# Feed-forward blocks of a four-layer kernel: a step's down products moved between its gate products and its up products

## The chip, the cores and the metric

One core of one Trainium2 chip runs the whole program. The metric is the device time of one execution in microseconds (us); the kernel before was run three times. The engines are TensorE (PE, with its weight loads as PEld), VectorE (DVE), ScalarE (ACT), GpSimd (POOL) and SyncE (SP), which here only issues DMAs.

## The reference, cut to what matters

The program computes four layers, each a cross-attention and then a feed-forward block, on x of 4 x 256 tokens by 256 features in float32. A feed-forward block is, on the normalised input h,

```python
g = h @ w_gate          # 1024 tokens x width
u = h @ w_up
y = (silu(g) * u * gate_of_the_expert) @ w_down   # layer 3: silu(g * u) for the routed experts
x = x + y
```

Layer 0 is dense with 704 hidden features. Layers 1, 2 and 3 are mixtures in which all experts are computed and laid side by side: 64 experts of 64 features and a shared one (4160), 8 experts of 176 and a shared one of 704 (2112), 16 experts of 176 and a shared one of 176 (2992). An expert's gate is zero where it isn't chosen for a token.

## The kernel before

**Tiles and steps.** The hidden features are cut into chunks of 128: 6, 33, 17 and 24 chunks in the four blocks. The 1024 tokens are cut into two halves of 512. A *step* st is one chunk and one half (c = st // 2, h = st % 2), so the blocks have 12, 66, 34 and 48 steps, 160 in all. Every float32 operand of a product is split into a high and a low float16 part, and a product is hi*hi + lo*hi + hi*lo.

**TensorE** (`pe_ffn`). Per step it issues three groups, all in one queue that runs in order:

- gate products g(st): 6 matmuls of 512 columns (lines 1217 to 1219) into bank h of the accumulator memory; they wait until `s.a` says that VectorE has read the gate products of two steps before;
- up products u(st): 6 matmuls of the same form into bank 2, the only bank for them. They wait until VectorE has read those of the step before (`s.prod`, or `s.a` where the product comes first);
- down products d(st - 8): 12 matmuls of 256 columns (lines 1238 to 1240) that add the hidden features of eight steps before (LAG = 8) into banks 4 to 7. They wait for the low part of these hidden features (`s.lo`) and, at even steps, for the down weights' low part (`s.dn_lo`).

The first eight steps have no down products; the last eight groups of them follow the loop as a tail. So 128 of the 160 groups of down products stand inside the loop.

**VectorE** (`dve_ffn`, `dve_front`) takes in each step st, in this order, with the line of each instruction: a(st) = (tanh + 1) * g (1351); the product with u, m_b (1355); the low part of the next chunk's up weights at even steps (1275), or of the down weights at odd steps (1288); and low(st - 7), the low part of hidden features (1368, or 1370 without an expert gate), which d(st - 7) of the next step waits for. In the first 22 chunks of layer 3 the product comes first: a(st) = g * u (1348), then the weights' part, then, after ScalarE's tanh, m_b (1384), then low(st - 7).

**ScalarE** (`act_ffn`) takes tanh of the gate products (1308; in layer 3 a copy at 1304, and the tanh of a(st) at 1338), the high parts of the weights (1270, 1283) and the high part of the hidden features high(st - 7) (1318, 1321), which waits for the down products that read the same buffer two steps earlier (`s.down`).

**GpSimd** (`pool_ffn`, line 1408) multiplies m_b(st) by the expert's gate into m_c. It waits for m_b(st), for the gates' DMA at even steps, and for low(st - 2), whose buffer it overwrites.

**SyncE** issues the loads in a queue written out by hand: up weights five chunks ahead once `s.up_lo` frees a slot, the rows of gates, the down weights (`sp_ffn`). No planner sets the order; it is the order of the loops above.

Of the kernel before, what the change touches and what calls it, by code (L numbers as in the profile page):

```python
# [36 lines left out]
LAG = 8  # L37
# [47 lines left out]
def build(nc, d, out):  # L85
    ctx = ExitStack()
    with ctx:
# [1063 lines left out]
        def product_first(n, st):  # L1151
            return st // 2 < FFNS[n].first
# [57 lines left out]
        def pe_ffn(n):  # L1210
            pe, s, f = nc.tensor, ffn, FFNS[n]

            def up(c, h, u, to):
                for k in range(KT):
                    w_hi, w_lo = (up_w[:, c % 2, a, (2 * k + u) * P:(2 * k + u + 1) * P] for a in range(2))
                    x_hi, x_lo = (a[:, k, 4 * h:4 * h + 4, :].rearrange("p t c -> p (t c)") for a in (xh, xl))
                    pe.matmul(to, w_hi, x_hi, start=(k == 0), stop=False)  # L1217
                    pe.matmul(to, w_lo, x_hi, start=False, stop=False)  # L1218
                    ins = pe.matmul(to, w_hi, x_lo, start=False, stop=(k == KT - 1))  # L1219
                return ins  # L1220

            def gates_turned():
                pe.wait_ge(s.parts, n)
                for i in range(NT):
                    ins = pe.transpose(PS[0:f.experts, 6 + i // 4, (i % 4) * P:(i % 4 + 1) * P], gates[:, i, 0:f.experts], ident[:])
                ins.then_inc(s.gates_ps, 1)

            def down(st):
                c, h, last = st // 2, st % 2, st >= f.steps - 2
                if h == 0:  # L1230
                    pe.wait_ge(s.dn_lo, f.tiles0 + c + 1)
                pe.wait_ge(s.lo, f.steps0 + st + 1)
                w_hi, w_lo = (dn_w[:, c % 2, a, :] for a in range(2))
                for j in range(4):
                    i = 4 * h + j
                    to = PS[:, 4 + i // 2, (i % 2) * D:(i % 2 + 1) * D]
                    h_hi, h_lo = (hid[:, h, a, j, :] for a in range(2))
                    pe.matmul(to, h_hi, w_hi, start=(c == 0 and i % 2 == 0), stop=False)  # L1238
                    pe.matmul(to, h_hi, w_lo, start=False, stop=False)  # L1239
                    ins = pe.matmul(to, h_lo, w_hi, start=False, stop=(last and i % 2 == 1))  # L1240
                    if last and j == 1:
                        ins.then_inc(s.y_ps, 1)
                if last:
                    ins.then_inc(s.y_ps, 1)
                else:
                    ins.then_inc(s.down, 1)

            for st in range(f.steps):
                c, h = st // 2, st % 2
                if h == 0:  # L1250
                    pe.wait_ge(s.up_lo, f.tiles0 + c + 1)
                if st >= 2:
                    pe.wait_ge(s.a, f.steps0 + st - 1)
                up(c, h, 0, PS[:, h, :]).then_inc(s.g_ps, 1)
                if st >= 1:
                    pe.wait_ge(s.a if product_first(n, st - 1) else s.prod, f.steps0 + st)
                up(c, h, 1, PS[:, 2, :]).then_inc(s.u_ps, 1)
                if st == 3 and f.gated:
                    gates_turned()
                if st == LAG and f.gated:  # L1260
                    pe.wait_ge(s.gates, n)
                if st >= LAG:
                    down(st - LAG)
            for st in range(f.steps - LAG, f.steps):
                down(st)

# [797 lines left out]
        @block.tensor  # L2064
        def _(pe):
            pe_latent(0)
            pe_pre0()
            pe_ffn(0)
            pe_folded(1)
            pe_pre1(1, r1_w, E1 + 1)  # L2070
            pe_ffn(1)
            pe_folded(2)
            pe_pre2()
            pe_ffn(2)
            pe_latent(3)
            pe_pre1(3, r3_w, E3)
            pe_ffn(3)
# [199 lines left out]
```

## Time and profile before

| | |
|---|---|
| median of 3 runs | 1530.09 us (1529.9 to 1530.73) |
| profiled execution, its own time | 1534.58 us |
| its span in the trace | 1532.8 us |
| granted TensorE clock, mean | 0.915 of full speed |
| TensorE busy | 1297.8 us (85%) |
| VectorE busy | 925.9 us (60%) |
| ScalarE busy | 501.6 us (33%) |
| GpSimd busy | 358.9 us (23%) |

The trace is of one execution and its times are us from the span's start. A matmul's recorded duration overlaps the next matmul, so the time that a matmul takes from TensorE is read from start to start. In the timeline a row gives the start, the duration, the engine, the line, the operation, what it writes and reads, and in brackets the idle time before it and what ended it. The granted clock is 1.00 at 2.4 GHz and 0.50 at 1.2 GHz.

### The profile page before, as it was taken

Reading aid. Unit: us, or ns where it says so; the run is one execution under the profiler, and the core shown is the slowest. Engines: PE = TensorE matmul, PEld = TensorE weight load, DVE = VectorE, ACT = ScalarE, POOL = GpSimd, SP = SyncE. Lnnn points to the kernel's source line nnn. Section 1 sums busy time; section 2 is a strip of 40 time slices with the busy share of each in tenths; the row PEclk is TensorE's granted clock in tenths of the full one; section 3 lists DMA queues with packets and bytes.
Section 4 is the critical chain, followed back from the end, with each engine's and each line's share of the span. In section 5 each row is a group of like instructions: output and inputs, shape, how many; then the busy total and the mean of one; then the engine's idle time right before and its main releaser. Section 6 shows DMA issues by size and latency. Waiting matters only on the chain.

```text
span 1532.8 us, 20643 instructions
## 1 busy us (share of the span) xinstructions
PE 1297.8 (85%) x7770; PEld 842.8 (55%) x7772; DVE 925.9 (60%) x1706; ACT 501.6 (33%) x1105; POOL 358.9 (23%) x325
## 2 busy tenths in 40 slices
PE   4658939999879999996997766996999667699998
PEld 2335525799855666654654543565466433456655
DVE  3657665577747666667224448675666655576666
ACT  2322313111123333332221113563333223255553
POOL 0220030366502333333001121000133211123332
PEclk9887969999979999999898878798999977799999
DMA  3010024000024444451330000000234200034442
GB/s 122 1 72 2 27 86 151 1 1 1 1 74 113 116 117 120 121 131 52 117 118 0 0 14 0 1 1 1 81 115 129 94 14 0 1 98 120 121 134 73
DMA packets 41499, 97.53 MB, mean 64 GB/s; under 512 B 5414, under 2 KB 18214, under 8 KB 39360
## 3 DMA queue, kind: packets, MB, share of 16 engines
q1 hardware_dynamic: 41408, 96.31, 20.7%
q8 instruction: 57, 0.93, 0.3%
q14 instruction: 34, 0.28, 0.1%
HBM read 94.88 MB, written 1.42 MB: 63 GB/s over the span
## 4 chain that ended last, share of the span: by engine, by line
PE 61%; issue 21%; DVE 11%; POOL 4%; ACT 3%; DMA 1%; POOLq 0%; SPq 0%; DVEq 0%; ACTq 0%
PE PS L1217 9%; PE PS L1218 9%; PE PS L1219 9%; PE PS L1238 4%; PE PS L1240 4%; PE PS L1239 4%; PE PS L873 3%; POOL arena L323 2%; PE PS L891 2%; PE PS L1826 2%; PE PS L666 2%; PE PS L1843 1%; PE PS L860 1%; PE PS L862 1%; PE PS L861 1%
## 5 line engine op out<-in xcount | busy, mean ns | idle before, releaser
L1408 POOL TENSOR_TENSOR arena<-arena,m_g 128x512 f32<-128x512 f32 x144 | 184.3, 1281 | 441.9 <-DMA m_g<-gate_rows 259.4
L1217 PE MATMUL PS<-arena 128*128 128x512 f16 x640 | 245.8, 384 | 5.1 <-DVE arena L1348 2.2
L1218 PE MATMUL PS<-arena 128*128 128x512 f16 x640 | 245.6, 384 | 0.0
L1219 PE MATMUL PS<-arena 128*128 128x512 f16 x640 | 245.2, 383 | 0.0
L1238 PE MATMUL PS<-arena 128*128 128x256 f16 x640 | 174.5, 273 | 11.9 <-DVE arena L1368 10.2
L1240 PE MATMUL PS<-arena 128*128 128x256 f16 x640 | 174.4, 273 | 0.0
L1239 PE MATMUL PS<-arena 128*128 128x256 f16 x640 | 174.4, 273 | 0.0
L1351 DVE SCALAR_TENSOR_TENSOR arena<-arena,PS 128x512 f32<-128x512 f32 x116 | 79.6, 686 | 133.6 <-ACT arena L1308 133.6
L1308 ACT ACTIVATE arena<-PS 128x512 f32<-128x512 f32 x116 | 69.3, 597 | 263.5 <-PE PS L1219 263.5
L1368 DVE TENSOR_TENSOR arena<-arena 128x512 f16<-128x512 f32 x144 | 114.0, 792 | 2.2 <-ACT arena L1318 2.2
L323 POOL TENSOR_TENSOR arena<-arena,small 128x1024 f32<-128x1024 f32 x24 | 46.2, 1938 | 264.6 <-DVE small L479 264.6
L1219 PEld LDWEIGHTS PS<-arena 128*128 128x128 f16 x640 | 63.3, 99 | 77.6 <-issue 3.6
L1217 PEld LDWEIGHTS PS<-arena 128*128 128x128 f16 x640 | 63.7, 100 | 70.8 <-issue 3.3
L1218 PEld LDWEIGHTS PS<-arena 128*128 128x128 f16 x640 | 63.2, 99 | 62.4 <-issue 2.9
L937 POOL TENSOR_TENSOR arena<-arena 128x256 f32<-128x256 f32 x96 | 67.6, 726 | 125.6 <-DVE arena L965 125.6
L1318 ACT ACTIVATE arena<-arena 128x512 f16<-128x512 f32 x144 | 89.3, 620 | 22.3 <-PE PS L1240 20.7
L1355 DVE TENSOR_TENSOR arena<-arena,PS 128x512 f32<-128x512 f32 x116 | 79.7, 687 | 17.4 <-PE PS L1219 2.7
L1238 PEld LDWEIGHTS PS<-arena 128*128 128x128 f16 x640 | 62.5, 98 | 39.6 <-issue 10.6
L471 DVE TENSOR_REDUCE small<-PS 128x16 f32<-128x1024 f32 x24 | 29.2, 1215 | 85.0 <-PE PS L1012 38.0
L1239 PEld LDWEIGHTS PS<-arena 128*128 128x128 f16 x640 | 62.5, 98 | 20.3
L1240 PEld LDWEIGHTS PS<-arena 128*128 128x128 f16 x640 | 62.6, 98 | 7.3
L1275 DVE SCALAR_TENSOR_TENSOR arena<-w_stage,arena 128x512 f16<-128x512 f32 x80 | 64.2, 807 | 2.8 <-ACT arena L1270 2.8
(251 smaller groups left out, 2358.6 us busy)
## 6 DMA issues: line engine op xcount, KB each, us to landing
w_stage<-in_up SPq DMA_DIRECT2D x80, 256.0 KB, 2.8
m_g<-gate_rows SPq DMA_DIRECT2D x70, 256.0 KB, 4.3
arena<-in_heads SPq DMA_DIRECT2D x16, 1088.0 KB, 5.0
w_stage<-in_down SPq DMA_DIRECT2D x80, 128.0 KB, 4.1
m_g<-gate_rows SPq DMA_DIRECT2D x19, 512.0 KB, 3.8
m_g<-gate_rows SPq DMA_DIRECT2D x6, 448.0 KB, 4.6
m_g<-gate_rows SPq DMA_DIRECT2D x6, 384.0 KB, 4.2
m_g<-gate_rows SPq DMA_DIRECT2D x6, 320.0 KB, 4.0
```

Of the source, the lines that this page charges most:

```text
L323: pool.tensor_tensor(heads_of(at_p[:, q, :]), heads_of(at_p[:, q, :]), over(small[:, q, 2, :], 2, L), ALU.mult).then_inc(norm.pn, 1)
L1217: pe.matmul(to, w_hi, x_hi, start=(k == 0), stop=False)
L1218: pe.matmul(to, w_lo, x_hi, start=False, stop=False)
L1219: ins = pe.matmul(to, w_hi, x_lo, start=False, stop=(k == KT - 1))
L1238: pe.matmul(to, h_hi, w_hi, start=(c == 0 and i % 2 == 0), stop=False)
L1239: pe.matmul(to, h_hi, w_lo, start=False, stop=False)
L1240: ins = pe.matmul(to, h_lo, w_hi, start=False, stop=(last and i % 2 == 1))
L1318: act.activation(hid_part(0, st % 2), m_c[:, st % 2, :], ACT.Copy).then_inc(s.hi, 1)
L1351: dve.scalar_tensor_tensor(a, t, 1.0, g_ps, ALU.add, ALU.mult).then_inc(s.a, 1)
L1355: dve.tensor_tensor(m_b[:, st % LAG, :], a, u_ps, ALU.mult).then_inc(s.prod, 1)
L1368: dve.tensor_tensor(hid_part(1, st % 2), m_c[:, st % 2, :], hid_part(0, st % 2), ALU.subtract).then_inc(s.lo, 1)
L1408: pool.tensor_tensor(m_c[:, st % 2, :], m_b[:, st % LAG, :], m_g[:, st // 2 % 2, st % 2, :], ALU.mult).then_inc(s.c, 1)
```

## The change

In every step of every feed-forward block, the down products of eight steps before are issued between the gate products and the up products, and not after the up products. With them go their waits, and in step 8 the wait for the transposed gates. In step 3 the transposition of the gates keeps its place after the up products. No instruction is added or removed on any engine, and only TensorE's queue is reordered.

```diff
@@ -1252,15 +1252,15 @@
                 if st >= 2:
                     pe.wait_ge(s.a, f.steps0 + st - 1)
                 up(c, h, 0, PS[:, h, :]).then_inc(s.g_ps, 1)
+                if st == LAG and f.gated:
+                    pe.wait_ge(s.gates, n)
+                if st >= LAG:
+                    down(st - LAG)
                 if st >= 1:
                     pe.wait_ge(s.a if product_first(n, st - 1) else s.prod, f.steps0 + st)
                 up(c, h, 1, PS[:, 2, :]).then_inc(s.u_ps, 1)
                 if st == 3 and f.gated:
                     gates_turned()
-                if st == LAG and f.gated:
-                    pe.wait_ge(s.gates, n)
-                if st >= LAG:
-                    down(st - LAG)
             for st in range(f.steps - LAG, f.steps):
                 down(st)
```

## Rows read from the trace of the kernel before

**Rows 1.** Stretches in us: length, busy PE, PEld, DVE, ACT, POOL, clock, DMA share, GB/s.

```profile
475.00:700.00 225.00, 224.66 (x1380) 134.73 (x1378) 146.35 (x231) 87.76 (x173) 76.58 (x60) 1.00 0.45 119
1357.00:1512.00 155.00, 153.77 (x944) 91.98 (x942) 99.46 (x160) 82.88 (x154) 51.44 (x41) 1.00 0.40 120
702.70:717.50 14.80, 11.56 (x96) 8.84 (x96) 13.79 (x15) 4.83 (x10) 7.74 (x6) 1.00 0.22 65
```

**Rows 2.** TensorE's timeline, layer 1, step 41: u, d, next g.

```profile
605.80 0.38 PE L1217 MATMUL PS<-arena 128*128 128x512 f16 x1
...
607.10 0.27 PE L1238 MATMUL PS<-arena 128*128 128x256 f16 x1
...
608.41 0.38 PE L1217 MATMUL PS<-arena 128*128 128x512 f16 x1
```

**Rows 3.** The timeline of VectorE, layer 1, steps 41 and 42.

```profile
606.63 0.69 DVE L1351 SCALAR_TENSOR_TENSOR arena<-arena,PS 128x512 f32<-128x512 f32 x1 [0.77 <-ACT arena L1308]
607.45 0.69 DVE L1355 TENSOR_TENSOR arena<-arena,PS 128x512 f32<-128x512 f32 x1
608.06 0.42 DVE L1288 SCALAR_TENSOR_TENSOR arena<-w_stage,arena 128x256 f16<-128x256 f32 x1
608.39 0.69 DVE L1368 TENSOR_TENSOR arena<-arena 128x512 f16<-128x512 f32 x1
...
611.35 0.69 DVE L1355 TENSOR_TENSOR arena<-arena,PS 128x512 f32<-128x512 f32 x1
611.96 0.68 DVE L1275 SCALAR_TENSOR_TENSOR arena<-w_stage,arena 128x512 f16<-128x512 f32 x1
612.56 0.68 DVE L1368 TENSOR_TENSOR arena<-arena 128x512 f16<-128x512 f32 x1
```

**Rows 4.** TensorE's and VectorE's timelines, layer 3, step 24 (product first).

```profile
1423.61 0.27 PE L1238 MATMUL PS<-arena 128*128 128x256 f16 x1
...
1423.89 0.69 DVE L1348 TENSOR_TENSOR arena<-arena,PS 128x512 f32<-128x512 f32 x1 [1.15 <-PE PS L1219]
...
1425.95 0.68 DVE L1368 TENSOR_TENSOR arena<-arena 128x512 f16<-128x512 f32 x1
```

**Rows 5.** The timeline where layer 1's tail begins: VectorE, TensorE, GpSimd.

```profile
701.99 0.68 DVE L1368 TENSOR_TENSOR arena<-arena 128x512 f16<-128x512 f32 x1
702.87 1.79 DVE L1368 TENSOR_TENSOR arena<-arena 128x512 f16<-128x512 f32 x1 [0.19 <-ACT arena L1318]
...
700.70 0.27 PE L1238 MATMUL PS<-arena 128*128 128x256 f16 x1
...
702.82 0.27 PE L1238 MATMUL PS<-arena 128*128 128x256 f16 x1 [0.65 <-DVE arena L1368]
...
702.85 1.27 POOL L1408 TENSOR_TENSOR arena<-arena,m_g 128x512 f32<-128x512 f32 x1 [2.99 <-DVE arena L1368]
```

**Rows 6.** TensorE's timeline, first down products of layers 1, 0, 3.

```profile
478.40 0.27 PE L1238 MATMUL PS<-arena 128*128 128x256 f16 x1 [0.34 <-DVE arena L1368]
...
165.76 0.27 PE L1238 MATMUL PS<-arena 128*128 128x256 f16 x1
...
1359.14 0.39 PE L1217 MATMUL PS<-arena 128*128 128x512 f16 x1 [0.62 <-DVE arena L1348]
1361.22 0.27 PE L1238 MATMUL PS<-arena 128*128 128x256 f16 x1 [0.61 <-DVE arena L1368]
```

**Rows 7.** VectorE's timeline, layer 0, step 7: the low part.

```profile
164.44 0.69 DVE L1370 SCALAR_TENSOR_TENSOR arena<-arena 128x512 f16<-128x512 f32 x1
```

**Rows 8.** The timeline of VectorE and GpSimd, layer 1, from step 40.

```profile
604.16 1.10 DVE L1275 SCALAR_TENSOR_TENSOR arena<-w_stage,arena 128x512 f16<-128x512 f32 x1
...
610.69 1.28 POOL L1408 TENSOR_TENSOR arena<-arena,m_g 128x512 f32<-128x512 f32 x1 [3.42 <-DMA m_g<-gate_rows]
```

**Rows 9.** TensorE's timeline, layer 0, first gate products.

```profile
140.83 0.63 PE L1218 MATMUL PS<-arena 128*128 128x512 f16 x1
141.26 0.63 PE L1219 MATMUL PS<-arena 128*128 128x512 f16 x1
```

## The prediction, made before the changed kernel was run

> **What bounds the kernel now.** I read the page first (TensorE 85% busy, the others at 60% or less), then the view by stretches of the loops, then the timeline of TensorE and of VectorE side by side over single steps. In the loops TensorE is never without work: 224.66 of 225.00 us in layer 1, 153.77 of 155.00 in layer 3, at the full clock of 2.4 GHz [rows 1]. A step is read from start to start: an up group takes 1.30 us (605.80 to 607.10), a down group 1.31 (607.10 to 608.41) [rows 2], and the gate group, of the same form as the up group, makes the step 3.90, which is also the distance of VectorE's product from step to step (607.45 to 611.35) [rows 3]. No wait inside the loop costs anything, so there is no stall to win back. What must be seen beside this is how late VectorE is. After the up products of an odd step (issued by 607.10) the low part that the *next* down products need starts only at 608.39 and ends at 609.08; after an even step (611.00, one step later) it starts at 612.56 [rows 3]. TensorE does not notice, because between these up products and the down products that read the low part stand d, g and u: 3.91 us.
>
> **The change, part by part.** Work is the same on every engine, and no DMA moves. Between two up groups there are still one d and one g, so the wait for the single up bank has its old cover of 2.61 us. The gate banks' wait has its old cover too. What shrinks is the cover of the down group: between u(st) and d(st - 7), which needs low(st - 7), now stands g(st + 1) alone, 1.30 us. And low(st - 7) stays in VectorE's queue behind the product with u(st). So a circle closes in each step: u ends, VectorE takes the product, a weights' part and the low part, TensorE does d, then u again.
>
> The circle's terms. (a) From u's last slot to VectorE's start: 0.28, as in layer 3 (1423.61 to 1423.89) [rows 4]. In layer 1 it is 0.35 (607.10 to 607.45), but there the product also waits for a(st), which ended at 607.32 [rows 3]; with u 1.31 later a(st) is early, and I take 0.28. The bounds are 0.28 and 0.35. (b) Product to weights' part 0.61; weights' part to low part 0.33 at odd steps (608.06 to 608.39), 0.60 at even ones (611.96 to 612.56) [rows 3]. (c) Start of the low part to the start of the down group that waited for it: 0.83, seen where the tail begins (701.99 to 702.82) [rows 5]. (d) d and u: 2.61. An odd step is then 0.28 + 0.61 + 0.33 + 0.83 + 2.61 = 4.66, 0.76 more than 3.90. An even one is 0.28 + 0.61 + 0.60 + 0.83 + 2.61 = 4.93, 1.03 more. The last even step of a block has no up weights to split: 0.28 + 0.61 + 0.83 + 2.61 = 4.33, 0.43 more. Where the product comes first (layer 3, steps up to 43), ScalarE's tanh lies in the chain, and u's end to the low part's start is 2.34 (1423.61 to 1425.95) [rows 4]: 2.34 + 0.83 + 2.61 = 5.78, 1.88 more. The tail gives a check of the odd chain: from 700.70, where u ended, to 702.82, where a down group waited for the low part, is 2.12 [rows 5]; my sum with 0.35 in place of 0.28 is 2.12.
>
> Counts. The circle runs from u(8) to the last u, in blocks of S steps S - 9 times: 3, 57, 25 and 39. Layer 0: 1.03 + 0.76 + 0.43 = 2.2. Layer 1: 28 x 1.03 + 28 x 0.76 + 0.43 = 50.6. Layer 2: 12 x 1.03 + 12 x 0.76 + 0.43 = 21.9. Layer 3: 36 x 1.88 + 1.03 + 0.76 + 0.43 = 69.9. Together 144.6 us.
>
> The first down group, once per block. In layers 1 and 3 d(0) already waits for its low part (478.40, 1361.22) [rows 6], so it starts when it did. Before, u(8) was already done by then and g(9) came next; now u(8) follows d(0) and ends 2.61 (d and u) after d(0)'s start, the point from which the turns above are counted: +2.61. I take the same for layer 2. In layer 0, d(0) started at 165.76, and its low part at 164.44 would let it start at 165.27: 2.61 - 0.49 = 2.12 [rows 6, 7]. Sum 3 x 2.61 + 2.12 = 10.0. The wait for the gates in step 8 costs nothing: ScalarE copies them in step 4, and d(0) waits longer for its low part. The tail's chain starts at the last u as before, 0.07 earlier by term (a): 0.3 in all four.
>
> **Sum:** 144.6 + 10.0 - 0.3 = +154.3 us. The profiled execution of 1534.58 (its span is 1532.8, 1.8 around it) would become 1688.9; it lies 4.5 above the median of 1530.09, to which I apply the same sum: **1684.4 us**. Other queues: `s.down` now comes before u, so ScalarE's high parts are not later; SyncE's loads follow VectorE's and GpSimd's progress, and a longer step gives them more room. Later layers wait for this one's x, so nothing behind it absorbs the delay.
>
> **A cost that was hidden: VectorE beside GpSimd.** Where the gates' product ran (702.85, 1.27 us), the low part took 1.79 instead of 0.68 [rows 5]; 1275 took 1.10 once [rows 8]. Products that read PSUM stayed at 0.69 [rows 3, 4]. In the loop before, such a hit vanished in the slack; now it would sit on the circle. The Trainium skill has this as a lock ("SBUF — State Buffer", section "SBUF: two separate sides"): a VectorE instruction with two SBUF inputs and a GpSimd one that reads SBUF exclude one another for a whole instruction. The rows agree; the drawn-out 1.79 is such a case. I price it at zero in the sum: GpSimd starts either after the low part that frees its buffer, or 5.43 us after the end of 1275 (605.26 to 610.69) [rows 8]. In the new step, 1275 ends at 0.28 + 0.61 + 0.68 = 1.57, so the gates' product starts at 7.00 after an even u, 2.07 into the next step. That is after its low part (1.22 to 1.90), and GpSimd is done at 3.35, before the next u ends at 4.66. The bound above is 1.11 at every other step.
>
> **Rivals.**
> - *Collisions come back.* If the gates' DMA lands otherwise than I put it, GpSimd's 1.28 us falls on 1275 or the low part. Up to 1.11 x 40 even steps of layers 1 and 2 = +44: 1728 at most, half of it 1706. For it: rows 5 and 8. Against: 2 us of room. Chance 0.08.
> - *The clock falls.* TensorE will rest 1.87 of every 5.78 us in layer 3 (3.17 less g's 1.30) and 0.75 to 1.02 of some 4.8 in the others. In layer 1's tail it was 11.56 of 14.80 us busy, and the clock was granted at 1.00 throughout [rows 1], so I expect full clock. At 1.2 GHz a matmul of 512 columns takes 0.43 (140.83 to 141.26) [rows 9] against 0.217, d and u 5.2 instead of 2.61: 2.6 more per step, +47 if half of layer 3's 36 product-first steps fall there: 1731, and more if other layers join. The Trainium skill states such a rule against this change ("TensorE: Matmul & The Clock Gate", section "A second HAM failure mode: psum-queue depth-cycling"): frequent short idles between groups of matmuls can make the clock swing between its levels. The tail's rows contradict it for its own pattern; no row has 1.87 us of rest in each step. Chance 0.08.
> - *Not slower.* The point is the wait for the low part in front of d: it costs nothing if the low part starts by 1.30 - 0.83 = 0.47 us after u's end. Then g covers it, and only the one wait before u(8) in layer 3 (0.62 [rows 6]) might go: 1529.5, no change. Against: it starts at 1.29 at the earliest [rows 3], and VectorE's order is fixed with the product ahead of it. Chance 0.02.
> - *A circle only partly closed*, with hand-overs shorter than read, or half the steps stalling: +60 to +130, 1590 to 1660. No row supports it. Chance 0.03. That the change does nothing can't be: TensorE's products run in the order written.
>
> **How the numbers follow.** Forecast 0.79, rivals 0.08, 0.08, 0.02, 0.03. Errors of 0.1 us in the circle give 12 us over its 124 turns; with (a) at 0.35 the sum is +163 at most. The lower end allows 0.15 per turn: 1665. The upper end takes in most of the collisions: 1722. A measurement of this kernel can tell 0.2% (3.1 us) from no change. Faster by more than that 0.01, within it 0.02, slower 0.97.
>
> **What would show it.** In the changed profile: TensorE's idle time before line 1238 grows to 120 to 145 us and is ended by 1368; a step in layer 1 lasts 4.66 and 4.93 by turns, in layer 3 5.78; the loops of layers 1 and 3 are 53 and 72 us longer; PEclk stays at 1.00; 1275 and 1368 keep medians of 0.68. The prediction is wrong if the step stays near 3.9, if 1238 waits for something else, or if 1217 to 1219 start 0.43 apart.

## The result and the profile after

| | before | changed |
|---|---|---|
| median | 1530.41 us (4 runs, 1529.90 to 1540.68) | 1675.82 us (4 runs, 1673.69 to 1681.64) |
| profiled execution, its own time | 1534.58 us | 1681.64 us |
| its span | 1532.8 us | 1679.9 us |

The ratio of the changed kernel to the kernel before is 1.0939, with a 95% interval of 1.0884 to 1.0994. The changed kernel is slower by 145 us between the medians, and by 147.1 us between the two profiled executions. The forecast was 154.3 us more, 1684.4 us in all, with a range of 1665 to 1722.

The page of the changed kernel, its costliest groups: where TensorE and VectorE stood idle, and what ended it.

```profile
PE 1321.3 (79%) x7772; PEld 833.6 (50%) x7772; DVE 916.1 (55%) x1706; ACT 498.8 (30%) x1105; POOL 359.7 (21%) x325
...
L1238 PE MATMUL PS<-arena 128*128 128x256 f16 x640 | 174.8, 273 | 136.7 <-DVE arena L1368 131.3
L1217 PE MATMUL PS<-arena 128*128 128x512 f16 x640 | 246.2, 385 | 4.8 <-DVE arena L1427 2.1
...
L1355 DVE TENSOR_TENSOR arena<-arena,PS 128x512 f32<-128x512 f32 x116 | 79.7, 687 | 203.1 <-PE PS L1219 200.7
```

The matmuls cost what they did: 273 and 385 ns each, against 273 and 384 on the page before. What is new is idle time in front of the down products: 136.7 us, of which 131.3 are ended by VectorE's low part (1368). On the page before this entry read 11.9. In turn VectorE's product (1355) now waits 200.7 us for the up products. Each of the two waits for the other, which is how a closed circle looks on the page.

The stretches view of the changed kernel, with the columns of [rows 1]: the loops of layers 1 and 3.

```profile
475.00:700.00 225.00, 194.03 (x1138) 107.58 (x1136) 118.21 (x193) 73.72 (x145) 60.94 (x48) 1.00 0.38 100
1445.00:1650.00 205.00, 145.62 (x859) 81.09 (x858) 88.79 (x145) 73.64 (x144) 44.86 (x36) 1.00 0.27 80
```

TensorE was busy for 224.66 of 225 us in layer 1 before and now for 194.03. In layer 3 it is busy for 71% of the stretch. The clock stays at 1.00 in both.

The timeline of the changed kernel, layer 1, one even and one odd step (TensorE's up group ended at 592.14, the next one at 596.96 and the one after at 601.59).

```profile
594.34 0.28 PE L1238 MATMUL PS<-arena 128*128 128x256 f16 x1 [0.75 <-DVE arena L1368]
595.66 0.38 PE L1217 MATMUL PS<-arena 128*128 128x512 f16 x1
598.98 0.27 PE L1238 MATMUL PS<-arena 128*128 128x256 f16 x1 [0.57 <-DVE arena L1368]
600.29 0.38 PE L1217 MATMUL PS<-arena 128*128 128x512 f16 x1
...
592.39 0.69 DVE L1355 TENSOR_TENSOR arena<-arena,PS 128x512 f32<-128x512 f32 x1 [2.07 <-PE PS L1219]
593.00 0.69 DVE L1275 SCALAR_TENSOR_TENSOR arena<-w_stage,arena 128x512 f16<-128x512 f32 x1
593.60 0.68 DVE L1368 TENSOR_TENSOR arena<-arena 128x512 f16<-128x512 f32 x1
...
597.21 0.69 DVE L1355 TENSOR_TENSOR arena<-arena,PS 128x512 f32<-128x512 f32 x1 [2.26 <-PE PS L1219]
597.81 0.42 DVE L1288 SCALAR_TENSOR_TENSOR arena<-w_stage,arena 128x256 f16<-128x256 f32 x1
598.15 0.69 DVE L1368 TENSOR_TENSOR arena<-arena 128x512 f16<-128x512 f32 x1
```

Beside [rows 3] VectorE's sequence is the same and its durations are the same. But the down group, which stood 3.91 us behind the up products there, now waits at the end of the sequence. The chain of work that ended last, in order of time over the even step, walks the circle once: up products, product, weights' part, low part, down products, up products. Its columns are start, length, engine and line.

```profile
592.39 0.69 DVE arena L1355
593.08 0.60 DVE arena L1275
593.68 0.61 DVE arena L1368
594.29 0.04 issue
594.34 0.28 PE PS L1238
...
596.90 0.23 PE PS L1219
...
597.21 0.69 DVE arena L1355
```

In layer 3's product-first steps the circle is longer, as ScalarE's tanh lies in it. The timeline of the changed kernel, VectorE and then TensorE, in an even step:

```profile
1567.21 0.69 DVE L1348 TENSOR_TENSOR arena<-arena,PS 128x512 f32<-128x512 f32 x1 [3.02 <-PE PS L1219]
...
1568.67 0.69 DVE L1384 SCALAR_TENSOR_TENSOR arena<-arena 128x512 f32<-128x512 f32 x1 [0.17 <-ACT arena L1338]
1569.28 0.69 DVE L1368 TENSOR_TENSOR arena<-arena 128x512 f16<-128x512 f32 x1
...
1570.02 0.28 PE L1238 MATMUL PS<-arena 128*128 128x256 f16 x1 [1.62 <-DVE arena L1368]
```

Where the 147.1 us went, from the first and last matmul of each block in the two timelines:

The forecast of a block is its turns and its first down group, without the 0.1 us that its tail was to be shorter.

| block | before | changed | difference | forecast |
|---|---|---|---|---|
| layer 0 | 50.9 | 54.6 | +3.7 | +4.3 |
| layer 1 | 267.8 | 315.6 | +47.8 | +53.2 |
| layer 2 | 141.1 | 163.4 | +22.3 | +24.5 |
| layer 3 | 196.1 | 267.8 | +71.7 | +72.5 |

That is 145.5 us in the blocks. The other 1.6 us are a net: between the blocks of layers 1 and 2 the changed kernel took 4.7 us less, in the other stretches outside the blocks 6.3 us more. The instructions there are the same, and the runs of one kernel differ by more than that.

### The profile page after: what moved, and what is told of

It reads as the page before. It is cut to its first block, busy times and chain, and to the rows that moved or that the text cites. A ratio compares the mean times of both kernels' runs of the same rounds, so it can differ in the third digit from the quotient of the medians.

```text
span 1679.9 us, 20645 instructions
## 1 busy us (share of the span) xinstructions
PE 1321.3 (79%) x7772; PEld 833.6 (50%) x7772; DVE 916.1 (55%) x1706; ACT 498.8 (30%) x1105; POOL 359.7 (21%) x325
## 4 chain that ended last, share of the span: by engine, by line
PE 46%; DVE 24%; issue 21%; ACT 4%; POOL 4%; DMA 0%; DVEq 0%; POOLq 0%; SPq 0%; ACTq 0%
DVE arena L1368 5%; PE PS L1238 5%; PE PS L1219 5%; PE PS L1217 5%; PE PS L1218 5%; DVE arena L1355 4%; PE PS L1240 4%; PE PS L1239 4%; PE PS L873 2%; POOL arena L323 2%; PE PS L891 2%; DVE arena L1348 2%; DVE arena L1275 2%; DVE arena L1384 2%; PE PS L666 1%
## 5 line engine op out<-in xcount | busy, mean ns | idle before, releaser
L1238 PE MATMUL PS<-arena 128*128 128x256 f16 x640 | 174.8, 273 | 136.7 <-DVE arena L1368 131.3
L1355 DVE TENSOR_TENSOR arena<-arena,PS 128x512 f32<-128x512 f32 x116 | 79.7, 687 | 203.1 <-PE PS L1219 200.7
L1238 PEld LDWEIGHTS PS<-arena 128*128 128x128 f16 x640 | 62.1, 97 | 209.6 <-DVE arena L1368 93.1
L1368 DVE TENSOR_TENSOR arena<-arena 128x512 f16<-128x512 f32 x144 | 108.2, 753 | 3.0 <-ACT arena L1318 3.0
L1219 PEld LDWEIGHTS PS<-arena 128*128 128x128 f16 x640 | 63.4, 99 | 77.8 <-issue 4.1
L1217 PEld LDWEIGHTS PS<-arena 128*128 128x128 f16 x640 | 63.9, 100 | 69.9 <-issue 4.0
L1218 PEld LDWEIGHTS PS<-arena 128*128 128x128 f16 x640 | 63.3, 99 | 62.2 <-issue 3.2
L1348 DVE TENSOR_TENSOR arena<-arena,PS 128x512 f32<-128x512 f32 x44 | 30.2, 687 | 114.9 <-PE PS L1219 114.9
L1338 ACT ACTIVATE arena<-arena 128x512 f32<-128x512 f32 x44 | 27.8, 632 | 147.2 <-DVE arena L1348 147.2
L1240 PEld LDWEIGHTS PS<-arena 128*128 128x128 f16 x640 | 62.4, 98 | 7.5
```

What stands on the lines that cost most here:

```text
L1355: dve.tensor_tensor(m_b[:, st % LAG, :], a, u_ps, ALU.mult).then_inc(s.prod, 1)
L1368: dve.tensor_tensor(hid_part(1, st % 2), m_c[:, st % 2, :], hid_part(0, st % 2), ALU.subtract).then_inc(s.lo, 1)
```

## The experiments

My theory was the closed circle: the down group waits for a low part that stands in VectorE's queue behind the product with the up products before it. Rival A was that the place between gate and up products costs by itself (a bank's wait, or the switch from one kind of matmul to the other). Rival B was VectorE's total work. Where two runs of one kernel are given instead of an interval, there were only two.

**One step later.** The order stays, but the down products are those of nine steps before.

```diff
-                if st >= LAG:
-                    down(st - LAG)
+                if st >= LAG + 1:
+                    down(st - LAG - 1)
...
-            for st in range(f.steps - LAG, f.steps):
+            for st in range(f.steps - LAG - 1, f.steps):
```

> The down products keep their new place between gate and up products, but are those of nine steps before, so they need a low part that VectorE finished a whole step earlier; the tail has nine groups. My theory (the down group waits for the low part that stands in VectorE's queue behind the product with the last up products): the wait is gone, a step is 3.90 us again, idle before line 1238 falls from 137 to about 20 us, total 1528 to 1534. Rival A (the place between gate and up products costs by itself, by a bank's wait or by switching the kind of matmul): steps stay at 4.6 to 5.8, total about 1676.

Measured: 1533.03 us over 10 runs against 1534.05 for the kernel before on the same chip, ratio 1.0003 (0.9975 to 1.0031). After the ninth step every step lasts 3.90 us. The stretches view of this run, the same two loops as in [rows 1]:

```profile
475.00:700.00 225.00, 225.00 (x1383) 135.09 (x1381) 142.84 (x232) 95.07 (x174) 75.68 (x60) 1.00 0.46 119
1357.00:1512.00 155.00, 154.39 (x947) 92.48 (x946) 101.01 (x161) 80.68 (x157) 51.77 (x41) 1.00 0.41 120
```

Its page's entry for the down group:

```profile
L1238 PE MATMUL PS<-arena 128*128 128x256 f16 x640 | 174.5, 273 | 10.6 <-DVE arena L1368 8.9
```

The totals can't be told apart. With the groups in the changed order, but with data that is one step older, the whole loss is gone. Rival A falls: the place costs nothing.

**Down products first.** The group is moved ahead of the gate products, so that nothing stands between u(st) and d(st - 7).

```diff
+                if st >= LAG:
+                    down(st - LAG)
                 if st >= 2:
                     pe.wait_ge(s.a, f.steps0 + st - 1)
                 up(c, h, 0, PS[:, h, :]).then_inc(s.g_ps, 1)
-                if st >= LAG:
-                    down(st - LAG)
```

> The down products of eight steps before stand ahead of the gate products, directly behind the last step's up products. Between two up groups there are still one gate and one down group. My theory: no cover is left between u(st) and d(st - 7), so a step is low part's hand-over 2.03 (odd) or 2.21 (even) plus 3.91 = 5.94 and 6.12 us in layers 0 to 2, and 3.1 + 3.9 = 7.0 in layer 3's product-first steps: 1.30 us more than the change on each of 124 turns, total 1676 + 161 + about 5 at the starts = 1835 to 1845. Rival A (the up bank's wait, whose cover is the same 2.61 as in both kernels): no difference from the change, 1676, or from before, 1530.

Measured: 1964.16 and 1966.74 us, ratio 1.283. The direction and the place are as expected: the idle time before 1238 is 310.5 us. But the total is 120 to 130 us above my number. The steps of layer 1 show two kinds: 6.02 and 6.21 us, near the 5.94 and 6.12 expected, and among them others of 7.7 to 7.9. In layer 3 the product-first steps last 6.98 and 7.06, as expected, in some stretches, and 8.3 to 8.8 in others. The timeline of TensorE in a long step of layer 1:

```profile
656.63 0.40 PE L1238 MATMUL PS<-arena 128*128 128x256 f16 x1 [2.14 <-DVE arena L1368]
657.25 0.42 PE L1238 MATMUL PS<-arena 128*128 128x256 f16 x1
```

The stretches view of the same run, the loops of layers 1 and 3 and a part of layer 3's:

```profile
510.00:890.00 380.00, 265.61 (x1343) 142.47 (x1342) 136.39 (x223) 84.71 (x167) 70.84 (x56) 0.90 0.25 67
1640.00:1943.00 303.00, 193.49 (x919) 100.41 (x916) 92.73 (x152) 80.49 (x151) 48.05 (x38) 0.86 0.19 56
1635.00:1672.00 37.00, 20.34 (x120) 11.37 (x120) 13.88 (x24) 11.83 (x22) 6.33 (x5) 1.00 0.25 75
```

Three down matmuls take 0.62 us here (656.63 to 657.25) against 0.33 at the full clock (12 in 1.31 [rows 2]): that is 1.2 GHz. After 2.14 us without a matmul the clock was low for about 3 us, and in layer 1 this came back in every second or third step. Counted against the full-clock steps (6.02 and 6.21, 6.98 and 7.06), the longer steps of the four blocks cost 96 us. So most of the excess is this clock, which in my forecast for the change was a rival and in this experiment came true. Of the remaining 25 to 35 us, some 6 are the profiled execution of the changed kernel, which lies that far above the 1676 from which I had counted, and 8 lie between the blocks. The others are later first down groups, and full-clock steps 0.1 us longer than I had put them.

The length of the rests alone does not decide it. In the third stretch, a part of layer 3's loop, the recorded rests were 2.91 and 3.00 us by turns, longer than in layer 1, and the clock was granted at 1.00 for 37 us. What decides stays open.

**Layer 3 alone in the new order.**

```diff
-                if st >= LAG:
+                if st >= LAG and n == 3:
                     down(st - LAG)
...
+                if st >= LAG and n < 3:
+                    down(st - LAG)
```

> The new order in layer 3's block alone. My theory: layer 3's block lasts 267.8 us as in the changed kernel, the others as before (50.9, 267.8, 141.1), total 1530.4 + 71.7 = 1602. If the blocks share a cost (a clock that falls and stays low), it differs from 1602 by more than 8 us.

Measured: 1598.90 and 1611.45 us, median 1605.17, where 1602 was expected; the two runs differ by 12.6 us, so the total alone says little. The block of layer 3 lasts 267.6 us, the other three 50.9, 267.3 and 141.6. The blocks' costs add up: none depends on the others.

**VectorE's low part first.** TensorE keeps the changed order. In layers 0 to 2 VectorE takes the weights' part and the low part ahead of a(st) and the product.

```diff
+                early = n < 3 and st >= LAG
-                if begun <= st < f.steps:
+                if begun <= st < f.steps and not early:
                     dve_front(n, st)
...
                 if st >= LAG - 1:
                     low(st - LAG + 1)
+                if begun <= st < f.steps and early:
+                    dve_front(n, st)
```

> The changed order on TensorE, and in layers 0 to 2 VectorE takes the weights' part and the low part ahead of a(st) and the product with the up products, from step 8 on. Layer 3 is as in the changed kernel. My theory: the low part no longer stands behind the product that waits for the up products, the circle is open, and the three blocks are back at 3.90 us per step (51, 268 and 141 us, within 3 each): total 1676 - 3.7 - 47.8 - 22.3 = 1602. Rival A (TensorE's order costs by itself): no gain, 1676. Rival B (VectorE as a whole is too slow for the step): no gain, since its work is the same.

Measured: 1614.53 and 1614.62 us, ratio 1.054. The three blocks last 51.1, 267.7 and 141.9 us and the steps in them after the ninth 3.90 each; layer 3 keeps its 268.0. The total is 12 us above the 1602 expected. The blocks account for about 1 us of this. Some 6 are again the distance of the changed kernel's profiled execution from the 1676 used, and 5.4 lie outside the blocks, 4.9 of them between the blocks of layers 1 and 2 (last section). The timeline of VectorE in this run, after an up group that ended at 570.86:

```profile
570.22 0.68 DVE L1368 TENSOR_TENSOR arena<-arena 128x512 f16<-128x512 f32 x1
570.82 0.68 DVE L1351 SCALAR_TENSOR_TENSOR arena<-arena,PS 128x512 f32<-128x512 f32 x1
571.63 0.69 DVE L1355 TENSOR_TENSOR arena<-arena,PS 128x512 f32<-128x512 f32 x1
```

The low part ends at 570.90, before the product (571.63), and the down group started at 572.15 right behind the gate group. VectorE's work is the same, so rival B falls too. It is the queue's order that closes the circle.

**The up weights' part behind the low part**, at even steps that aren't product-first; this measures one term of the sum.

```diff
+                late = st >= LAG and not (st < f.steps and product_first(n, st))
-                if h == 0 and 2 <= c + 1 < f.tiles:
+                if h == 0 and 2 <= c + 1 < f.tiles and not late:
                     dve_up_lo(n, c + 1)
...
                     low(st - LAG + 1)
+                if h == 0 and 2 <= c + 1 < f.tiles and late:
+                    dve_up_lo(n, c + 1)
```

> The changed order, and at even steps from 8 on VectorE takes the up weights' part behind the low part and not ahead of it (layer 3's product-first steps unchanged, where that part lies in the shadow of the tanh). My theory, term (b): the circle of an even step loses 0.60 us, 4.82 becomes 4.22, odd steps stay at 4.63; 28 + 12 + 1 + 1 = 42 such steps, total 1676 - 25 = 1651. If the weights' part is not on the circle: 1676.

Measured: 1657.17 us (4 runs), ratio 1.0806 (1.0782 to 1.083). Even steps last 4.22 and odd ones 4.63, to the hundredth as expected. Layers 1 and 2 last 299.4 and 156.5 us, 16.2 and 6.9 less than in the changed kernel. The four blocks together are 24.2 us shorter and the profiled executions differ by 25.6, where 25 was expected; the median is 6 us above the 1651.

**One wait fewer.** The down group of an even step no longer waits for the weights' low part by itself.

```diff
-                if h == 0:
-                    pe.wait_ge(s.dn_lo, f.tiles0 + c + 1)
                 pe.wait_ge(s.lo, f.steps0 + st + 1)
```

> The changed order without the down group's own wait for the weights' low part at even steps; the low part that it waits for anyway is later in VectorE's queue. The trace of the changed kernel shows 0.84 us from the low part's start to a down group of an even step (two waits) and 0.75 to one of an odd step (one wait). If the second wait costs the difference, both are 0.75, even-step groups come 0.08 us earlier, and the total falls by 0.08 x 62 = 5 us to about 1671. If the difference has another cause (what VectorE does just before), nothing changes in the trace.

Measured: 1680.61 us (4 runs), ratio 1.0935 (1.0909 to 1.0962). That is not the 5 us less: a total can't show 0.3% here. The trace does. Its timeline of VectorE and TensorE (lines from 1231 on stand two higher up than before, so 1366 is the low part and 1236 the down group):

```profile
590.03 0.69 DVE L1366 TENSOR_TENSOR arena<-arena 128x512 f16<-128x512 f32 x1
...
594.58 0.68 DVE L1366 TENSOR_TENSOR arena<-arena 128x512 f16<-128x512 f32 x1
...
590.77 0.28 PE L1236 MATMUL PS<-arena 128*128 128x256 f16 x1 [0.75 <-DVE arena L1366]
595.32 0.28 PE L1236 MATMUL PS<-arena 128*128 128x256 f16 x1 [0.48 <-DVE arena L1366]
```

The group of an odd step starts 0.74 us after the low part starts, that of an even step also 0.74. In the changed kernel above they were 0.74 (593.60 to 594.34) and 0.83 (598.15 to 598.98). The turns that end in an even step's group are 4.56 instead of 4.63 in layer 1, and 5.69 instead of 5.77 in layer 3. The four blocks together are 5.3 us shorter (54.2, 312.6, 163.0 and 266.3). Only a part of that is shown to be the wait: in layer 1 the turns give 2.0 of 3.0 us and the block's first steps the rest, and in layer 3 a stretch at the low clock hides the gain in the sum of the turns.

**Down products first, low part first.** The edit of the fourth experiment in the order of the second, to see whether the clock comes back with the rest gone.

> The down products ahead of the gate products, as in the 1965 us kernel, with VectorE's low part ahead of the product in layers 0 to 2. There the rest in front of the down group was 2.1 to 2.3 us in each step, and the steps were 6.02, 6.21 and 7.7 to 7.9, these last at a clock that fell. My theory: with the low part done before the up products end, the rest goes and the full clock with 1.00 comes back: steps 3.90 to 4.1, blocks of 51 to 52, 268 to 280 and 141 to 147 us in place of 62, 437 and 218, total about 1710 to 1730. If the order of the groups itself keeps the clock low, steps stay above 5.

Measured: 1827.57 and 1841.68 us, ratio 1.1949, some 100 to 130 us above my number. The clock did come back, as the stretches view of layer 1's loop shows:

```profile
510.00:790.00 280.00, 219.23 (x1295) 122.26 (x1294) 133.65 (x215) 81.86 (x161) 68.34 (x55) 1.00 0.34 90
```

No step there is at the low clock. In layer 3, whose order on VectorE the edit leaves alone, the mean granted clock was 0.84 from 1450 us on. But the steps of layers 0 to 2 last 5.09 and 5.31, not 3.90 to 4.1: I had overlooked a second circle. It is read from the timeline, and no run takes it away by itself. There ScalarE's high part stands behind the tanh of the gate products, and VectorE's low part waits for it:

```profile
616.25 0.60 ACT L1308 ACTIVATE arena<-PS 128x512 f32<-128x512 f32 x1 [3.68 <-PE PS L1219]
616.74 0.41 ACT L1283 ACTIVATE arena<-w_stage 128x256 f16<-128x256 f32 x1
617.04 0.62 ACT L1318 ACTIVATE arena<-arena 128x512 f16<-128x512 f32 x1
...
617.70 0.69 DVE L1368 TENSOR_TENSOR arena<-arena 128x512 f16<-128x512 f32 x1
...
618.54 0.27 PE L1238 MATMUL PS<-arena 128*128 128x256 f16 x1 [1.03 <-DVE arena L1368]
```

From the end of the gate products (616.04) to the down group is 2.50 us; with down and gate groups (2.61) that is 5.11, the step that was measured. Only the up group (1.30) lies beside it.

**The kernel before with VectorE's low part first**, the one candidate to beat both.

> The kernel before (down products after the up products), and VectorE takes the weights' part and the low part ahead of a(st) and the product, from step 8 on, in all steps that aren't product-first (the last four of layer 3 included). In the run with the changed order and this edit, layer 1's tail after the last up products was 14.68 us against 16.88 before. If that comes from the low part being done when the tail begins, each of the four tails is 2.1 us shorter and the steps stay at 3.90: 8 us less than before, ratio 0.995. If GpSimd's product now falls on VectorE's work and TensorE has to wait, or the tail's gain belongs to the changed order, there is no gain.

Measured: 1546.44 us (6 runs), ratio 1.007 (1.0043 to 1.0098): 0.7% slower than before, where 0.5% faster was expected. Layer 1's tail is shorter by 0.9 us and not 2.1. And even steps of layers 1 and 2 last 4.12 us, because the weights' part, now at the head of the queue, waits for ScalarE's high part of the weights (1270). The timeline of VectorE after the up group that ended at 569.24:

```profile
569.28 0.69 DVE L1275 SCALAR_TENSOR_TENSOR arena<-w_stage,arena 128x512 f16<-128x512 f32 x1 [1.72 <-ACT arena L1270]
569.89 0.69 DVE L1368 TENSOR_TENSOR arena<-arena 128x512 f16<-128x512 f32 x1
...
571.31 0.69 DVE L1355 TENSOR_TENSOR arena<-arena,PS 128x512 f32<-128x512 f32 x1
```

The product now starts 2.07 us after the up group and not 0.35. The next up group, which needs it, had 2.61 us of cover and starts 0.22 late (572.06). So the same four instructions in another order close the circle at the up bank. The order before leaves slack at both.

## Why the prediction was right, and where its terms were off

The mechanism was right. Its main term, the turns of the circle, was 5% too high.

- **What bounds the kernel, and that no stall can be won back.** Right: the kernel whose down products come one step later, at full cover, is no faster than before (1.0003).
- **The circle.** Right. Three experiments move only its links (data one step older; the low part ahead of the product; the weights' part behind it) and the steps follow: 3.90, 3.90, and 4.22 at even steps. The steps of layers 1 and 2 were 4.82 and 4.63 by turns (forecast 4.93 and 4.66), layer 3's 5.69 and 5.77 (forecast 5.78).
- **The excess of the sum, 154.3 against 145.5 in the blocks,** lies in the turns. From u(8)'s end to the last up group's end I count 13.5, 268.8, 117.6 and 220.4 us, 136.7 more than their 124 turns at 3.90; forecast 144.6. Term (c), 0.83 from the low part to the down group, was read at the tail's first group, an even step's, and used for all. For odd steps' groups it is 0.74, and the experiment that takes the second wait away shows why. That is 0.09 for each of 64 turns, 5.8 us. Term (a) was 0.25 in layers 0 to 2 and not 0.28, some 0.03 x 88 turns = 2.6 us. Against these 8.4 us one turn in layer 3 was 0.4 us too long (6.13, no cause shown), which leaves 8.0 of the 7.9 us between 144.6 and 136.7.
- **The first down groups.** Forecast 10.0, measured 2.0, 1.7, 2.6 and 3.8 = 10.1. That the sum fits is luck in part, since two errors cancel. In layer 1 d(0) did not start when it had, but 0.9 us earlier in its block. In layer 3 TensorE first stood still for 2.79 us, and its clock then fell; its up group took 2.51 us in place of 1.30, and this I had not counted. The granted clock over the 4 us from 1437 on was 0.62. The stretches view of the changed kernel:

```profile
1433.00:1437.00 4.00, 1.21 (x8) 0.53 (x7) 3.15 (x5) 2.15 (x4) 0.37 (x1) 1.00 0.69 197
1437.00:1441.00 4.00, 4.00 (x19) 1.98 (x17) 0.21 (x1) 0.00 (x0) 1.26 (x1) 0.62 0.00 0
```

and its timeline of TensorE, the first down group and then a matmul of the up group:

```profile
1436.65 0.27 PE L1238 MATMUL PS<-arena 128*128 128x256 f16 x1 [2.79 <-DVE arena L1368]
...
1439.19 0.63 PE L1217 MATMUL PS<-arena 128*128 128x512 f16 x1
```

- **The tails.** Forecast 0.3 shorter in all, measured 0.13 in layer 0 and 0.4 in each of the others, 1.3: the low part of the first tail group starts earlier, and the next group then doesn't wait.
- **The collisions,** priced at zero. Right in the loops: on the page 1368 has a mean of 753 ns against 792 before, and no 1275 from the ninth step on is over 0.69 us. GpSimd's product started at 2.0 to 2.9 us after an up group in layers 1 and 2, in the gap that I had worked out, and at 3.2 to 3.5 in layer 3's product-first steps. From the ninth step on it did in no loop fall beside an instruction of VectorE with two SBUF inputs. The only stretched instructions of layer 1 are at its start and in its tail, beside GpSimd's product, where the low part took up to 1.78 us in the tail. The rule of the Trainium skill on the shared port ("SBUF — State Buffer", section "SBUF: two separate sides") agrees with these rows.
- **The clock.** In the stretches of the loops above it stayed at 1.00, though TensorE rests up to 1.87 us of every 5.7 in layer 3, from start to start (1.71 as recorded). Behind the first steps of the blocks it fell once, in layer 3's ninth step. In the experiment with down products first it fell again and again, at recorded rests of 1.96 and 2.14 us in steps of 6. The rule of the Trainium skill on short idles between groups of matmuls ("TensorE: Matmul & The Clock Gate", section "A second HAM failure mode: psum-queue depth-cycling"), which I had set against the change, did not hold for the changed kernel's loops and did for that experiment.
- **The signals.** Idle time before 1238: 136.7, in the forecast 120 to 145. The releaser is as named, and so is PEclk in the loops. The steps are 0.01 to 0.11 us shorter than named, and the blocks of layers 1 and 3 are 48 and 72 us longer, not 53 and 72.

What stays open: the run-to-run spread of this program, which the kernel before has too and which hides terms under 0.3%; and what makes the clock fall after one rest and not after another.

## What to carry to other kernels

Moving a group of work on the busiest engine leaves the work of every engine as it was, but it changes how much stands between a product and the answer that a later group needs. So before a reorder, list each pair (what is produced, who waits for what comes of it) with the time of the links between them and the time of the work that covers it. Here 3.91 us of cover for links of 2.1 became 1.30. Where the cover fails, ask how far back the data comes from: one step more in the lag was worth the whole 9%. And an in-order queue on a second engine has the same property: putting its late item first opened one circle and closed another.

## What the runs showed of the hardware that I had not expected

- TensorE's granted clock fell after a single rest of 2.79 us (layer 3 of the changed kernel). In the run with layer 3 alone changed, the rest at the same place was longer and the clock stayed full. Its timeline row, and its stretches view from there on:

```profile
1354.79 0.27 PE L1238 MATMUL PS<-arena 128*128 128x256 f16 x1 [2.87 <-DVE arena L1370]
1354.80:1360.80 6.00, 4.38 (x27) 2.55 (x28) 2.58 (x4) 1.98 (x5) 1.51 (x2) 1.00 0.12 29
```

  With down products first, the clock fell in every second or third step of layer 1, at recorded rests of 1.96 and 2.14 us, and stayed full for 37 us of layer 3 at 2.91 and 3.00. It stayed full in the loops with rests of 1.62 and 1.71 us in every 5.7 us, and of 1.03 and 1.24 in every 5.2. With the clock low for a part of it, a step of 6.0 to 6.2 us became 7.7 to 7.9. The 96 us lost to the clock with down products first are two thirds of what the change of this case costs. So a forecast for a kernel with rests of 2 to 3 us on TensorE has to carry both outcomes.
- A further wait that had been met before was not free. The wait for the down weights' low part was met some 0.6 us before the low part of the hidden features was done (598.23 against 598.84 in the rows of the changed kernel). With it ahead of a down group, the group still started 0.08 to 0.09 us later than without it.
- The same code between the blocks of layers 1 and 2, mostly attention, took 355.3 us in the profiled execution of the kernel before, 350.7 in the changed one's and 345.3 in that with layer 3 alone changed. The granted clock over it was 0.86, 0.87 and 0.89. The stretches view of the kernel before and of that one:

```profile
717.60:1072.90 355.30, 281.94 (x1632) 186.21 (x1633) 189.80 (x372) 111.30 (x366) 35.82 (x35) 0.86 0.08 27
```

```profile
718.60:1063.90 345.30, 271.29 (x1633) 180.18 (x1633) 189.73 (x372) 111.39 (x366) 35.82 (x35) 0.89 0.08 28
```

  That alone is 10 us between executions of the same instructions, while the blocks whose order was the same (layers 0 to 2) agree to 0.5 us. Totals of one kernel also differ by 10 us. That this stretch is where they differ is likely but not shown, since each kernel has one trace.
